# Two mixes in one TensorE call, the decays' products as a call of their own, and new orders on five engines

## The chip, the cores and the metric

The kernel runs on one core of one Trainium2 chip. The metric is device time in microseconds (us): the median of several runs. The profile comes from one more execution. TensorE is PE in the rows (PEld its weight loads), VectorE DVE, ScalarE ACT, GpSimd POOL, SyncE SP.

## The reference

A cross-attention block without softmax on x and a context (8 batches of 256 rows of 512 columns), followed by an RWKV block with a recurrent state of 32 heads of 16:

```python
g_x = conv1x1(g_w, g_b, ctx); theta_x = conv1x1(theta_w, theta_b, x); phi_x = conv1x1(phi_w, phi_b, ctx)
y = (theta_x^T phi_x / N) g_x^T ; x = batchnorm(conv1x1(w_w, w_b, y)) + x
xa = ln(x); sx = shifted(xa) - xa
t = tanh((xa + sx * maa_x) @ maa_w1).reshape(B, L, 5, 32)
mw, mk, mv, mr, mg = t_j @ maa_w2[j]                  # the five "mixes"
xw, xk, xv, xr, xg = xa + sx * (maa_j + m_j)
w = exp(-exp(time_decay + tanh(xw @ decay_w1) @ decay_w2))
r, k, v = xr @ Wr.T, xk @ Wk.T, xv @ Wv.T ; g = silu(xg @ Wg.T)
step: out = r (faaaa * k v^T + s) ; s = k v^T + w * s    # over 256 positions
x = x + groupnorm(out) * g @ Wo.T
xc = ln(x) ; x = x + sigmoid(xr2 @ fWr.T) * (square(relu(xk2 @ fWk.T)) @ fWv.T)
```

All operands are float32, and every weight and activation stays float32 on TensorE.

## The kernel before

Each batch goes through three parts, and the names of the calls say which: a_ (the attention block, the first layer norm, the five mixes and the products with Wk, Wv, Wr, Wg), b_ (the recurrence) and c_ (Wo, the second layer norm and the last three products). The parts are pipelined: in a round of the steady part, TensorE works on a_phi_g to a_x1 of a coming batch, on the mixes and products of batch b1, on the recurrence of b2 and on c_ of b3 and b4. Rounds run for i = 3 to 7; before them stands fill(), behind them drain(). Nothing is scheduled by a planner: each engine has fill, iteration and drain written out by hand as a list of calls, each call waits on semaphores, and an engine runs its list strictly in that order. So a call that waits holds back all that stands behind it on its engine.

The recurrence works inside blocks of 16 positions by doubling (h = 1, 2, 4, 8). Each batch has 17 chunks g of 128 x 512 products: 0 and 1 are the diagonal, 2 is h = 1, 3 and 4 are h = 2, 5 to 8 are h = 4, 9 to 16 are h = 8. VectorE makes the products of chunks 0 to 2 (b_prod), GpSimd those of 3 to 16; three buffers of prod hold them. TensorE sums each by a matmul with ones16 into one of the two halves of CH (b_chunks), VectorE weighs the half with v (b_weigh) and reduces it. Between two values of h, VectorE multiplies RA by the decays (b_update_r) and GpSimd multiplies K (b_update_k). For these, b_wprod makes the products of decays over 2, 4 and 8 positions and over the block (wprod, wblock): four VectorE instructions, called inside b_chunks at g == 1.

A mix is four matmuls with 32 rows of maa_w2 (for mix g of low_w) and 32 rows of tanh values: step m takes row group m for column tiles 0 and 1, and row group (m + 2) % 4 for tiles 2 and 3 (MIX_ROWS), in the order 0, 2, 1, 3. All five mixes go to PSUM tensor PA. VectorE adds maa and multiplies by sx into xmix (a_mix on VectorE, mix_scaled), GpSimd adds xa (a_mix on GpSimd, mix_ready). a_ranks leaves its result in PB, from which ScalarE takes the tanh (tmix_ready). a_decay and a_decay2, the two products of the decays, write PB too.

At the start TensorE runs keep_warm (four matmuls on zeros, inside a_phi_g(0, 0)), the first half of the context's product (a_phi_g), setup (the transposition of the output weights, which needs bn_s from GpSimd and the scaling by VectorE), and the second half. ScalarE's setup scales Wo by a half. In the last batch the calls b_sums, b_reads, c_turn_y, c_wo, c_turn and c_key have a keep_warm ahead of them.

In the rows one float32 matmul is two records (LDWEIGHTS and MATMUL each), so that "x8" is four matmuls.

Of the kernel before, what the change touches and what calls it, by code (L numbers as in the profile page):

```python
# [10 lines left out]
P = 128  # L11
# [10 lines left out]
def build_xattn_rwkv(nc, x_d, ctx_d, shift_d, s0_d, chan_d, bnv_d, theta_b_d, pgb_d, thetaT_d, pgT_d, ww_d,  # L22
                     maa_w1_d, maa_w2_d, dec_w1_d, low_w_d, square_d, ident_d, ones16_d, half_d, out_d):
    B, L, C = x_d.shape
# [6 lines left out]
    DM, DD = 32, 64  # L31
# [16 lines left out]
    with ExitStack() as ctx:  # L48
# [216 lines left out]
        def _(sp):  # L265
# [64 lines left out]
            def fill():  # L330
                keep_x1(0)
                load_ahead_ctx(2)
                load_ahead_ctx(3)
                keep_x1(1)
                load_ahead_x(2)
                load_x(1)
                keep_x1(2)
                load_ahead_x(3)
                keep_x1(3)

            def iteration(i):
# [3 lines left out]
                load_ctx(f1)  # L345
                keep_x1(f2)
                bring_x1(b4)
                load_x(b1)

            def drain():  # L350
                store(4)
# [4 lines left out]
                keep_x1(7)  # L356
# [10 lines left out]
        def _(pe):  # L367
# [114 lines left out]
            def a_mix(a, step):  # L482
                if a is None:
                    return
                if step == 0:
                    pe.wait_ge(tmix_ready, 7 * (a + 1))
                else:
                    pe.wait_ge(mix_scaled, 10 * a + 2 * step)
                for ct in [0, 2, 1, 3]:
                    g, w2, t = MIX_ROWS[step][ct // 2]  # L490
                    rows = slice(DM * g, DM * (g + 1))
                    mm = pe.matmul(PA[:, ct * L:(ct + 1) * L], w2[rows, MIX_COL[step][ct] * P:(MIX_COL[step][ct] + 1) * P],  # L492
                                   t[rows], start=True, stop=True)
                mm.then_inc(mix_mm, 1)

# [14 lines left out]
            def a_decay(a):  # L510
                if a is None:
                    return
                pe.wait_ge(mix_ready, 10 * a + 2)
                for kt in range(CT):
# [220 lines left out]
            def fill():  # L735
                a_phi_g(0, 0)
                setup(0)
# [10 lines left out]
                a_wa(1)  # L748
                a_x1(1)
                a_ranks(0)  # L750
                a_mix(0, 0)
# [3 lines left out]
                a_mix(0, 1)  # L755
                a_decay2(0)
                a_att(2)
# [5 lines left out]
                a_mix(0, 3)  # L763
                a_value(0, 0)
# [5 lines left out]
                a_receptance(0, 1)  # L770
                a_receptance(0, 2)
                a_receptance(0, 3)
                a_theta(2)
                b_chunks(0, 0, 2)
                a_gate(0, 0)
                a_wa(2)
                b_chunks(0, 2, 3)
                a_turn(1)
                a_gate(0, 1)
                a_gate(0, 2)  # L780
                b_chunks(0, 3, 5)
                a_gate(0, 3)
                a_x1(2)
                b_chunks(0, 5, 6)
                a_ranks(1)
                b_chunks(0, 6, 8)
                a_mix(1, 0)
# [1400 lines left out]
```

## Time and profile before

| | us |
|---|---|
| median of 3 runs | 906.08 |
| lowest, highest | 904.01, 906.25 |
| the profiled execution | 905.25 |
| its span, first to last instruction | 903.2 |
| TensorE busy in the span | 861.3 (95%) |
| VectorE busy | 626.5 (69%) |
| ScalarE busy | 352.0 (39%) |
| GpSimd busy | 298.7 (33%) |
| TensorE's mean granted clock | 0.994 of full |

A timeline row reads: start in us, time from start to end, engine, line, operation, output <- inputs, shapes, count of records, and in brackets the idle time before it and who ended it. Matmuls are pipelined, so a group of them ends some 0.16 us after the next can start.

### The profile page before, as it was taken

To read this page: it belongs to the slowest core of one execution; us is meant where nothing else is said; L and a number is where in the kernel's file an instruction comes from. 1 tells how busy PE (TensorE), PEld (TensorE's weight loads), DVE (VectorE), ACT (ScalarE), POOL (GpSimd) and SP (SyncE) were. 2 spreads that over 40 slices of the span, in tenths; PEclk is the share of its full clock that TensorE was granted. 3 is DMA by queue.
4 is the path that set the end of the run, shared out by engine and by line. 5 is a ranking of instruction groups with operands and counts; after the bars stand their busy time and mean duration, and the time that the engine had idled before them with its cause. 6 is when DMAs were issued, how large, how long until landed. Compare 5 with 4: busy or idle time off the path is not lost. (4 is left out here: it accounts for less than half of the span.)

```text
span 903.2 us, 16352 instructions
## 1 busy us (share of the span) xinstructions
PE 861.3 (95%) x6490; PEld 583.7 (65%) x6490; DVE 626.5 (69%) x1110; ACT 352.0 (39%) x715; POOL 298.7 (33%) x281
## 2 busy tenths in 40 slices
PE   6699999899999999999998999999999999999997
PEld 4477568557764776557764686647866577368674
DVE  1465966897589926997379954899369966995341
ACT  1222145633462146433362343621464147236422
POOL 2043632373107520274105720166202831640000
PEclk9999999999999999999999999999999999999999
DMA  9730111000011000300003000020001000010010
GB/s 308 296 94 1 46 56 41 1 1 1 2 42 53 1 3 1 117 1 1 1 1 116 1 2 2 27 91 1 2 1 47 1 2 1 1 48 3 16 56 24
DMA packets 17020, 34.09 MB, mean 38 GB/s; under 512 B 2224, under 2 KB 3888, under 8 KB 16944
## 3 DMA queue, kind: packets, MB, share of 16 engines
q1 hardware_dynamic: 14048, 31.20, 10.1%
q10 hardware_dynamic: 2896, 1.84, 0.7%
q8 instruction: 52, 0.85, 0.4%
q14 instruction: 24, 0.20, 0.1%
HBM read 24.65 MB, written 8.39 MB: 37 GB/s over the span
## 5 line engine op out<-in xcount | busy, mean ns | idle before, releaser
L586 PE MATMUL CH<-prod,ones 128*128 128x512 f32 x272 | 140.2, 610 | 17.6 <-DVE av L1637 7.2
L2030 POOL TENSOR_TENSOR xmix<-xmix,xa 128x512 f32<-128x512 f32 x80 | 94.0, 1196 | 185.0 <-DVE xmix L1545 185.0
L2040 POOL TENSOR_TENSOR prod<-RA,K 128x512 f32<-128x512 f32 x112 | 133.5, 1214 | 51.1 <-DVE RA L1607 31.1
L1545 DVE SCALAR_TENSOR_TENSOR xmix<-PA,chan,sx 128x256 f32<-128x256 f32 x160 | 66.1, 475 | 57.5 <-PE PA L492 57.5
L1219 ACT ACTIVATE st<-av,half 32x512 f32<-32x512 f32 x64 | 74.6, 1166 | 40.0 <-DVE av L1682 38.6
L586 PEld LDWEIGHTS CH<-prod,ones 128*128 128x128 f32 x272 | 46.0, 189 | 59.2 <-issue 33.1
L1637 DVE TENSOR_TENSOR av<-CH,vT 128x512 f32<-128x512 f32 x112 | 76.4, 682 | 7.6 <-PE CH L586 7.0
L1643 DVE TENSOR_REDUCE yred<-av 128x64 f32<-128x512 f32 (+2 forms) x112 | 76.9, 686 | 3.9
L498 PE MATMUL PC<-sqb,sq_fWk 128*128 128x256 f32 x256 | 59.9, 381 | 0.9 <-DVE sqb L1761 0.9
L680 PE MATMUL PC<-sq_Wo,y 128*128 128x512 f32 x128 | 60.3, 601 | 0.3 <-DVE y L1725 0.3
L498 PEld LDWEIGHTS PB<-xmix,sq_Wk 128*128 128x128 f32 x256 | 48.5, 190 | 17.9 <-issue 12.4
L498 PE MATMUL PB<-xmix,sq_Wk 128*128 128x256 f32 x256 | 59.9, 379 | 0.0
L498 PE MATMUL PB<-xmix,sq_Wg 128*128 128x256 f32 x256 | 59.9, 382 | 0.0
L498 PE MATMUL PB<-xmix,sq_Wr 128*128 128x256 f32 x256 | 59.4, 383 | 0.0
L505 PE MATMUL PC<-sq_fWv,kk 128*128 128x512 f32 x128 | 59.0, 597 | 0.0
L498 PE MATMUL PB<-xmix,sq_Wv 128*128 128x256 f32 x256 | 58.9, 383 | 0.0
L505 PE MATMUL PC<-sq_fWr,sxc 128*128 128x512 f32 x128 | 58.2, 594 | 0.0
L498 PEld LDWEIGHTS PC<-sqb,sq_fWk 128*128 128x128 f32 x256 | 48.3, 190 | 14.2 <-issue 7.2
L2052 POOL TENSOR_TENSOR K<-K,W 128x512 f32<-128x512 f32 x8 | 12.0, 1498 | 137.5 <-DVE prod L1575 137.5
L498 PEld LDWEIGHTS PB<-xmix,sq_Wr 128*128 128x128 f32 x256 | 47.8, 190 | 13.0 <-issue 7.3
L498 PEld LDWEIGHTS PB<-xmix,sq_Wg 128*128 128x128 f32 x256 | 47.4, 190 | 11.1 <-issue 5.7
L498 PEld LDWEIGHTS PB<-xmix,sq_Wv 128*128 128x128 f32 x256 | 47.4, 190 | 8.2 <-issue 2.0
(162 smaller groups left out, 1397.0 us busy)
## 6 DMA issues: line engine op xcount, KB each, us to landing
x<-x_rows SPq DMA_DIRECT2D x11, 512.0 KB, 3.9
x<-in_x SPq DMA_DIRECT2D x8, 512.0 KB, 4.0
x_rows<-x SPq DMA_DIRECT2D x8, 512.0 KB, 5.2
out_x<-x SPq DMA_DIRECT2D x8, 512.0 KB, 3.0
ctx_t<-in_ctx SPq DMA_DIRECT2D x5, 512.0 KB, 4.9
y<-in_ctx SPq DMA_DIRECT2D x3, 512.0 KB, 8.2
sq_Wk<-in_square SPq DMA_DIRECT2D x1, 1024.0 KB, 13.3
sq_Wv<-in_square SPq DMA_DIRECT2D x1, 1024.0 KB, 16.7
```

Of the source, the lines that this page charges most:

```text
L498: mm = pe.matmul(out[:, mt * L:(mt + 1) * L], w[:, kt, mt * P:(mt + 1) * P], rhs[:, kt, :], start=(kt == 0), stop=(kt == CT - 1))
L505: mm = pe.matmul(out[:, t * C:(t + 1) * C], lhs[:, kt, t * P:(t + 1) * P], w[:, kt, :], start=(kt == 0), stop=(kt == CT - 1))
L586: pe.matmul(CH[:, (g % 2) * CHUNK:(g % 2 + 1) * CHUNK], ones16[:], prod[:, g % 3, :], start=True, stop=True).then_inc(chunk_mm, 1)
L680: mm = pe.matmul(PC[:, t * C:(t + 1) * C], y[:, t * C + kt * P:t * C + (kt + 1) * P], sq_w["Wo"][:, kt, :], start=(kt == 0), stop=(kt == C ...
L1219: act.activation(st[p, :, :, 32 * q:32 * q + S], src, ACT.Copy, scale=half[p, 0:1]).then_inc(st_ready, 1)
L1545: i = dve.scalar_tensor_tensor(xmix[:, SLOT_OF[name], ct, :], PA[:, ct * L:(ct + 1) * L], vec("maa_" + name, ct), sx[:, ct, :], ALU.add, A ...
L1637: dve.tensor_tensor(by_pair(dst, h), by_pair(src, h), v, ALU.mult).then_inc(av_ready, 1)
L1643: dve.tensor_reduce(yred[:, c * n:(c + 1) * n], by_pair(dst, h), AX.X, ALU.add).then_inc(red_ready, 1)
L2030: pool.tensor_tensor(m, m, xa[:, ct:ct + 2, 1:L + 1], ALU.add).then_inc(mix_ready, 1)
L2040: pool.tensor_tensor(by_pair(prod[:, g % 3, :], h), r, k, ALU.mult).then_inc(prod_pool, 1)
L2052: pool.tensor_tensor(ke, ke, wfactor(h, 1), ALU.mult).then_inc(K_up, 1)
```

## The change

1. a_first_mixes replaces TensorE's a_mix(., 0) and a_mix(., 1): mix w goes to PA as before, mix k to PB, and the eight matmuls are issued so that four follow each other on four different row groups. VectorE's a_mix takes step k from PB.
2. a_decay, which writes PB, waits in addition until VectorE has read both mixes (mix_scaled).
3. b_wprod is a call of its own in VectorE's list, in a round ahead of b_prod(b2, 0), and no longer inside b_chunks.
4. The lists of all five engines have another order in many places: among them TensorE's setup(0) ahead of a_phi_g(0, 0), a_ranks ahead of chunk 0, ScalarE's a_xa(0) ahead of a_att(1), VectorE's c_shift behind chunk 13, GpSimd's mix sums, and SyncE's context loads behind those of x.

```diff
@@ tensor @@
             def a_mix(a, step):
                 if a is None:
                     return
-                if step == 0:
-                    pe.wait_ge(tmix_ready, 7 * (a + 1))
-                else:
-                    pe.wait_ge(mix_scaled, 10 * a + 2 * step)
+                pe.wait_ge(mix_scaled, 10 * a + (2 if step == 2 else 2 * step))
                 for ct in [0, 2, 1, 3]:
-                    g, w2, t = MIX_ROWS[step][ct // 2]
-                    rows = slice(DM * g, DM * (g + 1))
-                    mm = pe.matmul(PA[:, ct * L:(ct + 1) * L], w2[rows, MIX_COL[step][ct] * P:(MIX_COL[step][ct] + 1) * P],
-                                   t[rows], start=True, stop=True)
+                    mm = mix_columns(PA, step, ct)
                 mm.then_inc(mix_mm, 1)
+
+            def mix_columns(out, step, ct):
+                g, w2, t = MIX_ROWS[step][ct // 2]
+                rows = slice(DM * g, DM * (g + 1))
+                return pe.matmul(out[:, ct * L:(ct + 1) * L], w2[rows, MIX_COL[step][ct] * P:(MIX_COL[step][ct] + 1) * P],
+                                 t[rows], start=True, stop=True)
+
+            def a_first_mixes(a):
+                if a is None:
+                    return
+                pe.wait_ge(tmix_ready, 7 * (a + 1))
+                for lo in range(2):
+                    for out, step in [(PA, 0), (PB, 1)]:
+                        for ct in [lo, lo + 2]:
+                            mm = mix_columns(out, step, ct)
+                        if lo:
+                            mm.then_inc(mix_mm, 1)
...
                 pe.wait_ge(mix_ready, 10 * a + 2)
+                pe.wait_ge(mix_scaled, 10 * a + 4)
...
             def fill():
+                setup(0)
                 a_phi_g(0, 0)
-                setup(0)
                 a_phi_g(0, 1)
...
+                a_ranks(0)
                 a_x1(1)
-                a_ranks(0)
-                a_mix(0, 0)
+                a_first_mixes(0)
@@ scalar @@
                 setup(0)
+                a_xa(0)
                 a_att(1)
                 a_theta(1)
-                a_xa(0)
@@ vector @@
+                src = PB if name == "k" else PA
                 for ct in range(CT):
-                    i = dve.scalar_tensor_tensor(xmix[:, SLOT_OF[name], ct, :], PA[:, ct * L:(ct + 1) * L],
+                    i = dve.scalar_tensor_tensor(xmix[:, SLOT_OF[name], ct, :], src[:, ct * L:(ct + 1) * L],
...
                 for g in range(lo, hi):
-                    if g == 1:
-                        b_wprod(u)
```

The orders that matter most, as the programs have them. First TensorE's beginning, up to the first attention product, before and then changed (keep_warm writes CH, setup turns tmix into PB, a_phi_g writes PA from ctx_t):

```order
1 L371 MATMUL CH<-dec 128x256 x4
2 L394 MATMUL PA<-pgT,ctx_t 128x256 x4
3 L732 MATMUL PB<-ident,tmix 128x128 x2
4 L394 MATMUL PA<-pgT,ctx_t 128x256 x4
5 L405 MATMUL PA<-zbuf 128x128 x4
```

```order
1 L744 MATMUL PB<-ident,tmix 128x128 x2
2 L371 MATMUL CH<-dec 128x256 x4
3 L394 MATMUL PA<-pgT,ctx_t 128x256 x8
4 L405 MATMUL PA<-zbuf 128x128 x4
```

The transposition came between the halves of the context's product and is now ahead of all.

TensorE in the first third of a round, from the turn of y (c_turn_y), before and then changed (CH<-prod is a chunk, PB<-zbuf a_ranks, PC<-sq_Wo c_wo, PB<-xmix,dec_w a_decay, PB<-dec a_decay2):

```order
277 L652 MATMUL PC<-ident,y 128x128 x4
278 L586 MATMUL CH<-prod,ones 128x512
279 L652 MATMUL PC<-ident,y 128x128 x4
280 L586 MATMUL CH<-prod,ones 128x512 x2
281 L473 MATMUL PB<-zbuf,maa_w 128x256 x4
282 L477 MATMUL PB<-zbuf,maa_w 32x128 x8
283 L586 MATMUL CH<-prod,ones 128x512
284 L680 MATMUL PC<-sq_Wo,y 128x512 x2
285 L492 MATMUL PA<-tmix,maa_w 128x256 x4
286 L680 MATMUL PC<-sq_Wo,y 128x512 x2
287 L586 MATMUL CH<-prod,ones 128x512 x2
288 L680 MATMUL PC<-sq_Wo,y 128x512 x2
```

```order
268 L664 MATMUL PC<-ident,y 128x128 x4
269 L473 MATMUL PB<-zbuf,maa_w 128x256 x4
270 L477 MATMUL PB<-zbuf,maa_w 32x128 x8
271 L598 MATMUL CH<-prod,ones 128x512 x2
272 L664 MATMUL PC<-ident,y 128x128 x4
273 L493 MATMUL PA<-tmix,maa_w 128x256 x2
274 L493 MATMUL PB<-tmix,maa_w 128x256 x2
275 L493 MATMUL PA<-tmix,maa_w 128x256 x2
276 L493 MATMUL PB<-tmix,maa_w 128x256 x2
277 L598 MATMUL CH<-prod,ones 128x512 x2
278 L692 MATMUL PC<-sq_Wo,y 128x512 x4
279 L598 MATMUL CH<-prod,ones 128x512 x2
```

The ranks are ahead of all chunks instead of behind the third, and the double mix stands before chunk 2; mix w alone stood between two parts of c_wo. In both lists a_decay comes next but is followed before by mix k (row 291) and c_wo, now by c_wo and a_decay2.

VectorE at the start of a round's recurrence, before and then changed (gate is a_gate, prod<-RA,chan,K products 0 and 1, xc and x c_out, yint<-CH the weighing of chunks 0 and 1, wprod and wblock b_wprod, RA<-RA,W b_update_r):

```order
388 L1556 SCALAR_TENSOR_TENSOR gate<-gate,PB 128x512 x2
389 L1569 SCALAR_TENSOR_TENSOR prod<-RA,chan,K 128x256 x4
390 L1780 SCALAR_TENSOR_TENSOR xc<-xc,PC 128x512
391 L1782 SCALAR_TENSOR_TENSOR x<-xc,x 128x512
392 L1575 TENSOR_TENSOR prod<-RA,K 128x512
393 L1623 TENSOR_TENSOR yint<-CH,vT 128x512
394 L1592 TENSOR_TENSOR wprod<-W 128x512
395 L1592 TENSOR_TENSOR wprod<-wprod 128x256
396 L1592 TENSOR_TENSOR wprod<-wprod 128x128
397 L1590 TENSOR_TENSOR wblock<-wprod 128x4x16
398 L1607 TENSOR_TENSOR RA<-RA,W 128x512
399 L1623 TENSOR_TENSOR yint<-CH,vT 128x512
```

```order
392 L1565 SCALAR_TENSOR_TENSOR gate<-gate,PB 128x512 x2
393 L1603 TENSOR_TENSOR wprod<-W 128x512
394 L1603 TENSOR_TENSOR wprod<-wprod 128x256
395 L1603 TENSOR_TENSOR wprod<-wprod 128x128
396 L1601 TENSOR_TENSOR wblock<-wprod 128x4x16
397 L1578 SCALAR_TENSOR_TENSOR prod<-RA,chan,K 128x256 x4
398 L1789 SCALAR_TENSOR_TENSOR xc<-xc,PC 128x512
399 L1791 SCALAR_TENSOR_TENSOR x<-xc,x 128x512
400 L1734 TENSOR_TENSOR y<-y,gate 128x512
401 L1584 TENSOR_TENSOR prod<-RA,K 128x512
402 L1634 TENSOR_TENSOR yint<-CH,vT 128x512
403 L1618 TENSOR_TENSOR RA<-RA,W 128x512
```

The four instructions on the decays moved from behind product 2 to ahead of product 0, and the first c_gate (y<-y,gate) ahead of product 2.

## Rows read from the trace of the kernel before

**Rows 1.** Windows: length, each engine's busy time (instructions), granted clock, DMA share, GB/s.

```profile
479.98:585.25 105.27, 102.98 (x797) 69.77 (x796) 77.72 (x138) 43.38 (x90) 36.67 (x35) 1.00 0.08 26
...
41.92:49.83 7.91, 7.91 (x24) 5.75 (x25) 1.66 (x4) 0.00 (x0) 2.31 (x2) 0.58 0.00 0
```

**Rows 2.** Groups by line, TensorE: busy us, mean ns, idle before and releasers.

```profile
L586 PE MATMUL CH<-prod,ones 128*128 128x512 f32 x272 | 140.2, 610 | 17.6 <-DVE av L1637 7.2 <-POOL prod L2040 6.6 <-DVE prod L1569 2.7
```

**Rows 3.** Timeline of TensorE in a round: chunk 3, mix w, c_wo, chunk 6.

```profile
484.93 1.12 PE L586 MATMUL CH<-prod,ones 128*128 128x512 f32 x2 [0.75 <-POOL prod L2040]
...
487.70 1.13 PE L492 MATMUL PA<-tmix,maa_w 32*128 32x256 f32 x8
488.76 1.98 PE L680 MATMUL PC<-sq_Wo,y 128*128 128x512 f32 x4
...
495.51 1.10 PE L586 MATMUL CH<-prod,ones 128*128 128x512 f32 x2 [1.33 <-DVE av L1637]
```

**Rows 4.** Timeline of TensorE, the first 15 us.

```profile
1.24 3.41 PE L371 MATMUL CH<-dec 128*128 128x256 f32 x8 [1.24 <-DVE dec L1821]
6.03 1.97 PE L394 MATMUL PA<-pgT,ctx_t 128*128 128x256 f32 x8 [1.38 <-DMA pgT<-in_pgT]
11.35 0.66 PE L732 MATMUL PB<-ident,tmix 128*128 128x128 f32 x2 [3.36 <-DVE bn_tmp L1792]
11.81 3.17 PE L394 MATMUL PA<-pgT,ctx_t 128*128 128x256 f32 x8
```

**Rows 5.** Timeline of ScalarE in the fill, 30 to 35 us.

```profile
30.06 1.91 ACT L1282 ACTIVATE sq_Wo<-sq_Wo 128x2048 f32<-128x2048 f32 x1 [10.16 <-DMA sq_Wo<-in_square]
...
32.70 1.93 ACT L1067 ACTIVATE xa<-PA,chan 128x256 f32<-128x256 f32 x4
```

**Rows 6.** Timeline of TensorE in the fill, 32 to 50 us.

```profile
32.19 0.70 PE L431 MATMUL PC<-wwT,sxc 128*128 128x256 f32 x2 [1.50 <-ACT sxc L1054]
...
36.48 1.99 PE L473 MATMUL PB<-zbuf,maa_w 128*128 128x256 f32 x8 [1.04 <-DVE zbuf L1526]
...
41.92 2.08 PE L492 MATMUL PA<-tmix,maa_w 32*128 32x256 f32 x8 [2.44 <-ACT tmix_g L1079]
43.92 5.97 PE L394 MATMUL PC<-pgT,y 128*128 128x256 f32 x16
```

**Rows 7.** Timeline of VectorE in a round, to the first c_gate, and c_shift.

```profile
475.39 1.67 DVE L1569 SCALAR_TENSOR_TENSOR prod<-RA,chan,K 128x256 f32<-128x256 f32 x4
477.59 0.69 DVE L1780 SCALAR_TENSOR_TENSOR xc<-xc,PC 128x512 f32<-128x512 f32 x1 [0.53 <-PE PC L505]
...
478.92 0.69 DVE L1575 TENSOR_TENSOR prod<-RA,K 128x512 f32<-128x512 f32 x1
...
480.12 1.70 DVE L1592 TENSOR_TENSOR wprod<-W 128x512 f32<-128x512 f32 x1
...
482.78 0.68 DVE L1607 TENSOR_TENSOR RA<-RA,W 128x512 f32<-128x512 f32 x1
...
483.99 1.43 DVE L1725 TENSOR_TENSOR y<-y,gate 128x512 f32<-128x512 f32 x1
...
510.93 1.50 DVE L1757 TENSOR_TENSOR sxc<-xc 128x1024 f32<-128x1024 f32 x1
512.47 2.36 DVE L1761 SCALAR_TENSOR_TENSOR sqb<-sxc,chan,xc 128x256 f32<-128x256 f32 x4
```

**Rows 8.** Timeline of GpSimd in a round: K's update, products 3 and 4, mix sum.

```profile
479.77 1.50 POOL L2052 TENSOR_TENSOR K<-K,W 128x512 f32<-128x512 f32 x1 [18.26 <-DVE prod L1575]
483.60 2.95 POOL L2040 TENSOR_TENSOR prod<-RA,K 128x512 f32<-128x512 f32 x2 [2.33 <-DVE RA L1607]
...
492.49 2.31 POOL L2030 TENSOR_TENSOR xmix<-xmix,xa 128x512 f32<-128x512 f32 x2 [1.41 <-DVE xmix L1545]
```

**Rows 9.** Timeline of TensorE at the last batch's chunks 3 and 5.

```profile
776.60 1.13 PE L586 MATMUL CH<-prod,ones 128*128 128x512 f32 x2 [0.39 <-POOL prod L2040]
...
781.47 1.12 PE L586 MATMUL CH<-prod,ones 128*128 128x512 f32 x2 [1.17 <-POOL prod L2040]
```

## What is predicted, and from what

> **What bounds the kernel now.** I read the windows first. A steady round of the pipeline lasts 105.27 us and TensorE is busy for 102.98 of it at the full clock, VectorE for 77.72 [rows 1]. So TensorE is the bound, and a round can only gain by less work on it or by its waits. The groups by line say where it waits: 17.6 us before the chunk matmuls, for VectorE's reading of the chunks, GpSimd's products and VectorE's [rows 2]. In a round two places make up nearly all of the 2.3 us that are left: 0.75 us before chunk 3, for GpSimd's product, and 1.33 us before chunk 6, for VectorE [rows 3]. The rest is the two ends. At the start TensorE waits until 11.35 us for the scaled output weights [rows 4], then from one engine's latency to the next up to 41.92 us, and after a wait of 2.44 us its clock falls to 1.2 GHz: of 41.92 to 49.83 us the mean granted clock is 0.58 [rows 1, 6].
>
> **The mixes.** One call of four 32-row matmuls (eight records) occupies TensorE from 487.70 to 488.76 us, 1.06 us [rows 3]; its two row groups run side by side, the other two lie idle. The new call puts the first two mixes, eight matmuls, on four groups. Low end: nothing saved, if only two groups run at a time, since no row of before shows four at this width. High end: 1.06 us, if the pair lasts as long as one call. I take 1.06, the row nearest to it: the call is made of the same stream, with groups that share nothing. No reason makes the pair longer than two calls, so there is no loss. Eight batches: -8.5 us.
>
> The Trainium skill (TensorE: Matmul & The Clock Gate, Part 3) gives 3.07 times, not 4, for four row groups at K=32 and 512 columns; by that figure the pair would last a tenth of a microsecond longer, an estimate of +0.5 us in all. No trace here shows it.
>
> **The start.** The transposition of the output weights now stands ahead of the four warming matmuls (3.41 us) and of both halves of the first context product. These used to fill the wait that ends at 11.35 us; now they follow it. Most of the warming runs at 1.2 GHz (0.43 us a record, as before), so it takes 3.0 us; the product's two halves then take 3.5 us at full clock instead of 3.17 for the second alone [rows 4]. TensorE is 3.4 us late at 15 us. It is given back: batch 1's chain had waits of 1.50 us (ScalarE scaled Wo until 31.97) and 1.04 us, ScalarE now puts xa(0) ahead of att(1), and the second a_x1 moves into the wait for the tanh [rows 5, 6]. Walked through, xa(0) starts at 32.4 us instead of 32.70, a_ranks(0) at 36.3 instead of 36.48, a_x1(1) runs from 39.1 to 40.9, and the mixes start at 41.7: -0.2 us. And TensorE then waits 0.8 us there instead of 2.44, so I take the clock to stay at 2.4 GHz: the mix costs 1.06 us instead of 2.00, and the context product 3.5 instead of 5.91: -3.4 us. Bounds of that: 0, if the clock falls all the same, and -3.4.
>
> **The middle.** I walk a round in the new order with the old durations, in us from the first c_turn_y (477.38 before). VectorE: products of the decays 2.66 (480.12 to 482.78), first products 1.6, c_out 1.33 (two rows of 0.69, start to start with what follows), c_gate 1.4 [rows 7]; product 2 is there at 5.6. GpSimd updates K until 7.3, and TensorE can take its first product 1.33 us after it started [rows 3, 8]: chunk 3 at 8.7. TensorE, with the ranks ahead of chunk 0 and the double mix behind, is there at 7.7: a wait of 0.9. Before the double mix it waits 0.3 for ScalarE's tanh. Next, a_decay has a new wait, since mix k lies in PB, which it overwrites: VectorE has read it at 15.2. But GpSimd, behind product 5, ends the sum of mix w (2.3 us) [rows 8] only at 15.9, and TensorE stands there at 14.9: 1.1. Behind this wait are queued c_wo, a_decay2 and chunk 6. Then 0.35 before chunk 12, and 1.0 before c_key, because c_shift (3.83 us) [rows 7] now comes after chunk 13 instead of chunk 10. That is 3.7 us of lost slots, 2.9 as the trace counts idle time, against 2.3: +0.6 a round, and four rounds make +2.4. The old waits go; the ones named are late next. The first round (b2 = 1) has no c_out to hide behind: its 2.7 us before chunk 0 [rows 2] becomes some 1.8, a new 1.2 appears in a_gate for mix g, and the others are as above: +1.3.
>
> **The drain.** With batch 6, VectorE goes through its 17 chunks without a pause, so TensorE's shorter mix is waited away again before b_turn_k: +1.1. For batch 7 the decays' products leave the chain, and 0.39 and 1.17 us before its chunks [rows 9] shrink: -1.2, with -1.6 and 0 as bounds. The last chain from the sums to the output has the same pieces, with two c_key ahead of the turn of K in place of behind: 0, within 1 us, covered by c_receptance. SyncE's moved loads (contexts behind x, keep_x1(7) earlier) are wanted tens of microseconds later: 0.
>
> **Sum.** -8.5 - 3.4 - 0.2 + 1.3 + 2.4 + 1.1 - 1.2 = -8.5 us. The profiled execution is 905.25 us, so 896.7; the median of the three runs, 906.08, is 0.8 higher, so I say 897.0.
>
> **Rivals.**
> A. Four groups don't overlap, the pair costs 2.1 us. For it: no row shows four. Against: two do so at no cost. 897.0 + 8.5 = 905.5, no change.
> B. The start isn't given back. If the tanh arrives 3.4 us late and the clock falls again, 897.0 + 3.4 + 3.4 = 903.8. For it: the walk hangs on ScalarE's order, where att(1) now stands behind xa(0). Against: 2.5 us of waits that only reappear if all of them are chained.
> C. Slower: the decays' products stand in front of the first chunk product. It decides as soon as TensorE arrives at chunk 0 before VectorE does; my walk leaves 1.7 us (product 0 ready at 1.55, TensorE at 3.3). If VectorE's gate comes later by more than that, each round pays up to 2.66 us [rows 7], five rounds 13.3: 910. Against: VectorE idles 0.53 us there now [rows 7], and ranks (2.7 us) cover the rest.
> D. Better: the waits that I found are hidden and the longer start of batch 1 gains as well. My walk of the fill gave another 2.5 us which I left out; with half of the waits gone, 889.
> That the table moves nothing is excluded by the order of instructions.
>
> **Numbers.** Forecast 897.0, 0.62; A 0.10; B 0.10; C 0.08; D 0.10. Range 889.5 to 904.5: it takes in B, half of D and the bounds of the unknown costs (0 to -3.4 for the clock, +-1 us a round for four walked rounds). A change of 0.3% (2.7 us) is about what a measurement of this kernel can tell from none. Faster than 903.4: forecast, D and a part of B, 0.77; within 0.3%: A and the rest of B, 0.14; slower: C and a tail, 0.09.
>
> **What would show it.** In PE's timeline the sixteen records of the double mix last 1.06 us (A: 2.1). The granted clock of 40 to 50 us is 1.0, and the mixes begin at 41.7 (B). Chunk 0 follows the ranks with no wait on VectorE's products (C). In a round the waits are before the double mix, chunk 3 (GpSimd), a_decay (GpSimd's xmix) and c_key (VectorE's sqb); a round lasts 104.8 us. I am wrong if a round is over 105.3 us, or if the clock still falls at 41.7 us.

## The result, and the profile after

| | before | after |
|---|---|---|
| median | 906.16 us (904.01 to 906.7, 4 runs) | 880.88 us (880.46 to 881.46, 4 runs) |
| ratio | | 0.9726, 95% interval 0.9709 to 0.9743 |
| the profiled execution | 905.25 us | 881.46 us |
| TensorE busy | 861.3 us | 846.3 us |
| VectorE, GpSimd busy | 626.5, 298.7 us | 613.3, 290.9 us |

The change gains 25 us. The forecast was 9 (897.0, range 889.5 to 904.5), so the direction held and the size did not. Among all the runs of this document two single executions, 2242 us in longer_products and 4955 us in scale_later, took several times as long as the others of their kernel, for a reason that no run shows; they move the two medians by some 0.2 us and leave scale_later without a trace to read. The stages below run from one first record of b_reads to the next in TensorE's timeline, the last one to the last matmul; the forecast column puts my terms where they belong.

| stage | before | after | change | forecast |
|---|---|---|---|---|
| fill | 152.6 | 147.6 | -5.0 | -0.2 - 3.4 - 2 x 1.06 = -5.7 |
| round i = 3 | 93.6 | 92.2 | -1.4 | +1.3 - 1.06 = +0.2 |
| round i = 4 | 106.8 | 102.5 | -4.4 | -0.5 |
| rounds 5 to 7, each | 105.27 | 102.45 | -2.8 | +0.6 - 1.06 = -0.5 |
| drain | 229.9 | 225.3 | -4.6 | +1.1 - 1.2 - 1.06 = -1.2 |

Between the two traces 23.8 us are gained where my terms make 8.5; the four rounds 4 to 7 hold 11 of the 15 us between them, the drain 3.4. (Round 4 before has one more wait, 1.34 us in b_sums, that the other rounds lack.) A round of after, as [rows 1] (length, TensorE busy, its weight loads, VectorE, ScalarE, GpSimd, clock, DMA share, GB/s):

```profile
463.80:566.24 102.44, 101.41 (x797) 69.30 (x796) 75.85 (x138) 43.68 (x89) 35.69 (x34) 1.00 0.08 27
```

Busy time fell by 1.57 us and idle time from 2.3 to 1.03. The group that had 17.6 us of waits in [rows 2]:

```profile
L598 PE MATMUL CH<-prod,ones 128*128 128x512 f32 x272 | 135.2, 602 | 1.7 <-DVE av L1648 1.4 <-POOL prod L2053 0.3
```

TensorE's timeline where [rows 3] stood:

```profile
469.57 0.48 PE L493 MATMUL PA<-tmix,maa_w 32*128 32x256 f32 x2
469.59 0.48 PE L493 MATMUL PB<-tmix,maa_w 32*128 32x256 f32 x2
...
470.33 0.38 PE L493 MATMUL PA<-tmix,maa_w 32*128 32x256 f32 x2
470.34 0.38 PE L493 MATMUL PB<-tmix,maa_w 32*128 32x256 f32 x2
470.65 1.98 PE L598 MATMUL CH<-prod,ones 128*128 128x512 f32 x4
472.47 3.60 PE L692 MATMUL PC<-sq_Wo,y 128*128 128x512 f32 x8
475.90 1.88 PE L598 MATMUL CH<-prod,ones 128*128 128x512 f32 x4
478.71 1.09 PE L528 MATMUL PB<-xmix,dec_w 128*64 128x128 f32 x16 [0.93 <-POOL xmix L2043]
```

The sixteen records of the pair start four at a time, 0.02 us apart, and the next call starts 1.08 us after them: one call's time for two. Chunks 2 and 3 (470.65) and 4 and 5 (475.90) follow with no wait. The only wait above 0.1 us in a steady round is the 0.93 before a_decay.

VectorE and GpSimd, as [rows 7] and [rows 8]:

```profile
461.80 0.69 DVE L1603 TENSOR_TENSOR wprod<-W 128x512 f32<-128x512 f32 x1
...
466.36 0.69 DVE L1734 TENSOR_TENSOR y<-y,gate 128x512 f32<-128x512 f32 x1
466.96 0.69 DVE L1584 TENSOR_TENSOR prod<-RA,K 128x512 f32<-128x512 f32 x1
...
468.83 1.04 DVE L1618 TENSOR_TENSOR RA<-RA,W 128x512 f32<-128x512 f32 x1
...
474.49 0.68 DVE L1618 TENSOR_TENSOR RA<-RA,wprod 128x512 f32<-128x512 f32 x1
...
487.22 0.53 DVE L1755 TENSOR_SCALAR sqb<-x,mv,rstd 128x512 f32<-128x512 f32 x1
...
492.95 1.00 DVE L1755 TENSOR_SCALAR sqb<-x,mv,rstd 128x512 f32<-128x512 f32 x1
...
499.14 1.21 DVE L1766 TENSOR_TENSOR sxc<-xc 128x1024 f32<-128x1024 f32 x1
500.39 1.67 DVE L1770 SCALAR_TENSOR_TENSOR sqb<-sxc,chan,xc 128x256 f32<-128x256 f32 x4
```

```profile
467.81 1.50 POOL L2065 TENSOR_TENSOR K<-K,W 128x512 f32<-128x512 f32 x1 [20.22 <-DVE prod L1584]
470.00 2.49 POOL L2053 TENSOR_TENSOR prod<-RA,K 128x512 f32<-128x512 f32 x2 [0.68 <-DVE RA L1618]
472.72 1.29 POOL L2065 TENSOR_TENSOR K<-K,wprod 128x512 f32<-128x512 f32 x1 [0.23 <-POOL prod L2053]
...
491.31 5.70 POOL L2053 TENSOR_TENSOR prod<-RA,K 128x512 f32<-128x512 f32 x5
```

This is where the forecast and the trace part. wprod<-W lasts 0.69 us; in [rows 7] it lasted 1.70. The first y<-y,gate lasts 0.69; there it lasted 1.43. In both traces every VectorE instruction that lasts over 0.15 us more than the shortest of its kind has a GpSimd instruction beside it, and the long tensor_tensor of 512 columns end some 0.55 us after it. wprod<-W of before starts at 480.12, 0.35 us into K<-K,W, which ends at 481.27; it ends at 481.82. RA<-RA,W here starts at 468.83 beside K<-K,W, which ends at 469.31, and ends at 469.87. So I read the long ones not as slow but as standing still until GpSimd is nearly done, and then taking their 0.69 us. Those with both inputs in SBUF do this. av<-CH,vT (one input in PSUM) does not, with a mean of 681 ns over 112 in after, and yred<-av (one input) neither, with 686. But one input is no safe sign: the TENSOR_SCALAR sqb<-x,mv,rstd, with x alone as a full input, lasts 0.53 us with GpSimd idle (487.22) and 1.00 beside GpSimd's products (492.95). The Trainium skill (SBUF — State Buffer, Who interferes with whom) says of two inputs just that: a VectorE instruction with two SBUF inputs contends with a GpSimd instruction that reads SBUF, and who starts first has the shared ports to its end. The traces agree, in both directions: GpSimd's products 3 and 4 take 2.49 us here and 2.95 in [rows 8], where y<-y,gate of [rows 7] ran in between.

The start, as [rows 4] and [rows 6], and ScalarE, as [rows 5]:

```profile
11.55 0.66 PE L744 MATMUL PB<-ident,tmix 128*128 128x128 f32 x2 [11.55 <-DVE bn_tmp L1801]
12.01 3.62 PE L371 MATMUL CH<-dec 128*128 128x256 f32 x8
15.42 4.41 PE L394 MATMUL PA<-pgT,ctx_t 128*128 128x256 f32 x16
21.14 1.16 PE L405 MATMUL PA<-zbuf 128*128 128x128 f32 x8 [1.32 <-DVE zbuf L1475]
...
37.74 1.99 PE L473 MATMUL PB<-zbuf,maa_w 128*128 128x256 f32 x8 [0.94 <-DVE zbuf L1534]
...
43.18 0.48 PE L493 MATMUL PA<-tmix,maa_w 32*128 32x256 f32 x2 [0.54 <-ACT tmix_g L1087]
...
44.26 3.72 PE L394 MATMUL PC<-pgT,y 128*128 128x256 f32 x16
```

```profile
30.30 1.91 ACT L1290 ACTIVATE sq_Wo<-sq_Wo 128x2048 f32<-128x2048 f32 x1 [5.56 <-DMA sq_Wo<-in_square]
...
33.96 1.92 ACT L1075 ACTIVATE xa<-PA,chan 128x256 f32<-128x256 f32 x4
```

TensorE comes 4.8 us late to the first attention product (16.30 before), the mixes 1.3 us late, and the context product behind them runs at full clock (3.72 us instead of 5.97). ScalarE's xa(0) is as late as the mixes (33.96 against 32.70).

The last batch's chunks 3 and 5, as [rows 9]; both waits are gone:

```profile
755.53 1.02 PE L598 MATMUL CH<-prod,ones 128*128 128x512 f32 x2
...
762.39 1.02 PE L598 MATMUL CH<-prod,ones 128*128 128x512 f32 x2
```

### The profile page after: what moved, and what is told of

Its sections match the earlier page's. It is cut to its first block, busy times and chain, and to the rows that moved or that the text cites. A ratio compares the mean times of both kernels' runs of the same rounds, so it can differ in the third digit from the quotient of the medians.

```text
span 879.4 us, 16360 instructions
## 1 busy us (share of the span) xinstructions
PE 846.3 (96%) x6490; PEld 578.6 (66%) x6490; DVE 613.3 (70%) x1110; ACT 354.1 (40%) x715; POOL 290.9 (33%) x281
## 4 chain that ended last, share of the span: by engine, by line
PE 84%; DVE 6%; issue 3%; ACT 3%; POOL 1%; DMA 1%; ACTq 0%; DVEq 0%; POOLq 0%
PE PB L509 24%; PE PC L516 13%; PE CH L598 9%; PE PC L509 6%; PE PC L692 4%; PE PA L493 4%; PE CH L657 3%; PE CH L634 3%; PE PB L371 2%; PE PA L394 2%; PE PB L473 2%; PE CH L452 2%; DVE xmix L1554 1%; PE PC L394 1%; PE PC L664 1%
## 5 line engine op out<-in xcount | busy, mean ns | idle before, releaser
L2043 POOL TENSOR_TENSOR xmix<-xmix,xa 128x512 f32<-128x512 f32 x80 | 96.7, 1230 | 170.1 <-DVE xmix L1554 170.1
L2053 POOL TENSOR_TENSOR prod<-RA,K 128x512 f32<-128x512 f32 x112 | 127.0, 1152 | 40.5 <-DVE RA L1618 32.4
L598 PE MATMUL CH<-prod,ones 128*128 128x512 f32 x272 | 135.2, 602 | 1.7 <-DVE av L1648 1.4
L1554 DVE SCALAR_TENSOR_TENSOR xmix<-PA,chan,sx 128x256 f32<-128x256 f32 x128 | 52.9, 475 | 35.3 <-PE PA L493 33.0
L598 PEld LDWEIGHTS CH<-prod,ones 128*128 128x128 f32 x272 | 47.9, 189 | 43.6 <-issue 31.3
L509 PEld LDWEIGHTS PB<-xmix,sq_Wk 128*128 128x128 f32 x256 | 48.1, 190 | 17.6 <-issue 12.5
```

The lines of the kernel that those rows point to most:

```text
L509: mm = pe.matmul(out[:, mt * L:(mt + 1) * L], w[:, kt, mt * P:(mt + 1) * P], rhs[:, kt, :], start=(kt == 0), stop=(kt == CT - 1))
L598: pe.matmul(CH[:, (g % 2) * CHUNK:(g % 2 + 1) * CHUNK], ones16[:], prod[:, g % 3, :], start=True, stop=True).then_inc(chunk_mm, 1)
L1554: i = dve.scalar_tensor_tensor(xmix[:, SLOT_OF[name], ct, :], src[:, ct * L:(ct + 1) * L], vec("maa_" + name, ct), sx[:, ct, :], ALU.add, ...
L2043: pool.tensor_tensor(m, m, xa[:, ct:ct + 2, 1:L + 1], ALU.add).then_inc(mix_ready, 1)
L2053: pool.tensor_tensor(by_pair(prod[:, g % 3, :], h), r, k, ALU.mult).then_inc(prod_pool, 1)
```

## The experiments

| kernel | median us | a round (i = 6), us |
|---|---|---|
| before (beside them) | 905.1 to 905.7 | 105.27 |
| after | 880.9 | 102.45 |
| mix_one_by_one | 881.0 | 102.46 |
| mix_apart | 884.6 | 102.69 |
| wprod_inside | 888.9 | 103.64 |
| orders_only | 892.9 | 103.64 |
| before_wprod | 902.6 | 104.65 |
| before_mix | 949.6 | 111.82 |
| before_small_K, after_small_K | 887.8, 874.0 | 103.04, 101.63 |
| longer_products | 889.2 | 104.05 |
| gate_back | 880.7 | 102.56 |
| decay_later, decay_later_x2 | 882.2, 882.0 | 102.83, 102.66 |
| mix_apart_decay_later | 886.1 | 102.96 |
| setup_between | 881.2 | 102.46 |
| scale_later, scale_later_v, mix_w_shared | 879.8, 881.9, 882.2 | -, 103.23, 103.06 |

### What the double mix is worth

In the order of issue of mix_one_by_one all of mix w stands ahead of all of mix k:

```diff
-                for lo in range(2):
-                    for out, step in [(PA, 0), (PB, 1)]:
-                        for ct in [lo, lo + 2]:
+                for out, step in [(PA, 0), (PB, 1)]:
+                    for ct in [0, 2, 1, 3]:
```

> The changed kernel with the two first mixes still in one call, but issued one mix after the other, so that two row groups run side by side and not four. If the pair on four groups is worth one call (1.06 us) and TensorE is the bound everywhere, the sixteen records last 2.1 us instead of 1.08 and the kernel takes 880.9 + 8 x 1.06 = 889.4 us. If waits of the new order take up the longer call (the 0.93 us before a_decay in five rounds), it is only some 885.

880.99 us: neither. TensorE's timeline:

```profile
468.36 0.48 PE L493 MATMUL PA<-tmix,maa_w 32*128 32x256 f32 x2
468.39 0.48 PE L493 MATMUL PB<-tmix,maa_w 32*128 32x256 f32 x2
...
469.45 1.13 PE L596 MATMUL CH<-prod,ones 128*128 128x512 f32 x2
```

In the records mix k's first matmuls start 0.03 us after mix w's first, though four matmuls of mix w were issued ahead of them, and the pair takes 1.09 us. The four row groups run together without the interleaved order; here it was enough that the two calls follow each other and share neither rows nor output. So this kernel did not take the overlap away, and mix_apart does it with work in between:

```diff
-                a_first_mixes(b1)
-                b_chunks(b2, 2, 4)
+                a_first_mix(b1, 0)
+                b_chunks(b2, 2, 3)
+                a_first_mix(b1, 1)
+                b_chunks(b2, 3, 4)
```

> The changed kernel with mix k issued behind the next piece of work (chunk 2, in the fill and the drain what follows there) instead of together with mix w, so that the two calls can't overlap: 8 x 1.06 us more work for TensorE. If every microsecond of TensorE's work counts, 880.9 + 8.5 = 889.4 us. My theory: in five rounds TensorE waits 0.93 us before a_decay for GpSimd's sum of mix w, whose moment does not depend on it, and the longer mix fills that wait: 5 x 0.13 + 3 x 1.06 = +3.8, 884.7 us.

884.59 us, as the theory said. TensorE's busy time in a round is 102.59 us instead of 101.41, and the wait before a_decay is gone from rounds 4 to 7:

```profile
472.15 1.13 PE L493 MATMUL PA<-tmix,maa_w 32*128 32x256 f32 x8
473.21 1.13 PE L595 MATMUL CH<-prod,ones 128*128 128x512 f32 x2
474.27 1.13 PE L493 MATMUL PB<-tmix,maa_w 32*128 32x256 f32 x8
...
481.54 1.09 PE L525 MATMUL PB<-xmix,dec_w 128*64 128x128 f32 x16
```

The pair saves 1.06 us of work eight times, but in the rounds TensorE then waits 0.93 us longer for GpSimd: of 8.5 us 3.7 reach the end. By stages of the two traces the fill has 2.2 us of it (149.8 against 147.6), rounds 4 to 7 have 0.24 each and the drain, though a pair stands there too, 0.2 (225.5 against 225.3).

before_mix gives the kernel before the double mix and a_decay's second wait, and no new order:

> The kernel before with only the double mix (and a_decay's wait for the reading of mix k), all orders as they were. TensorE has 8 x 1.06 = 8.5 us less work: 897.7 us if nothing else changes. But VectorE reads mix k only behind chunk 6, which TensorE issues right ahead of a_decay; a_decay then waits for VectorE from 496.5 to some 499.5 us of the old trace, 2.9 us in each of five rounds: theory 906.2 - 8.5 + 5 x 2.9 = 912 us. If the wait is hidden, 898.

949.6 us, 44 slower. The wait is where it was expected, and longer than the 2.9 us that I had given it:

```profile
527.03 1.98 PE L528 MATMUL PB<-xmix,dec_w 128*64 128x128 f32 x16 [5.00 <-DVE xmix L1554]
```

TensorE waits 5.00 us until VectorE, behind the weighing up to chunk 6, has read mix k, and a_decay runs at half clock after that (1.98 us instead of 1.09). The eight such waits come to 35.4 us, where I had expected five of 2.9, and the granted clock is 0.5 for 55.5 us of the span behind the start, against 11.6 in before. Alone the edit is a large loss; in the changed kernel, where VectorE reads mix k behind chunk 3, it is a gain.

### The products of the decays, and the orders

wprod_inside puts the four instructions back into b_chunks at g == 1:

```diff
                 for g in range(lo, hi):
+                    if g == 1:
+                        b_wprod(u)
...
-                b_wprod(b2)
                 b_prod(b2, 0)
```

> The changed kernel with the four products of the decays back inside b_chunks at g == 1, beside GpSimd's update of K. Theory (a VectorE instruction with both inputs in SBUF and GpSimd's instruction exclude each other): the first of the four takes 1.7 us again instead of 0.69, VectorE comes to product 5's RA and to mix w about 2.5 us later, TensorE's idle time in a round rises from 0.93 to 2.3 us or more, and the kernel takes 880.9 + 5 x 1.4 = 888 us. Rival (the new orders alone took the waits away, the place of the four does nothing): the first of them lasts 0.69 us and the kernel takes 881 +-1 us.

888.9 us: the size is right, the mechanism half. wprod<-W takes 0.68 us here, since it comes as K<-K,W is ending (574.09 and 574.20 us). But the four now stand between product 2 and RA, so product 3 comes 1.3 us later, and RA of h = 2 meets the second update of K:

```profile
577.87 1.13 PE L598 MATMUL CH<-prod,ones 128*128 128x512 f32 x2 [0.84 <-POOL prod L2051]
```

```profile
579.82 1.78 DVE L1618 TENSOR_TENSOR RA<-RA,wprod 128x512 f32<-128x512 f32 x1
```

A round is 1.2 us longer than in after, and the drain 3.3 us (228.6 against 225.3).

before_wprod moves them ahead of product 0 in the kernel before:

> The kernel before with only the four products of the decays moved ahead of product 0 on VectorE. Theory of the exclusion: the first of them takes 0.69 us instead of 1.70; product 2 comes some 0.9 us later and TensorE may wait up to 0.7 us for it, but the 0.75 us before chunk 3 and most of the 1.33 us before chunk 6 go: a round 1.0 to 1.5 us shorter, 906.2 - 5 x 1.2 = 900 us. Rival (my rival C: they stand in front of the first chunk and TensorE waits for it): a round up to 2.7 us longer, 906 to 919 us. Rival (the place does nothing alone): 906.

902.6 us (ratio 0.9975, 0.9964 to 0.9987), less than forecast. wprod<-W takes 0.69 us, but in the old order VectorE comes late to c_out (0.36 us before the second c_turn_y) and to the weighing of chunk 0 (0.44 us before chunk 2), RA<-RA,W stands beside K<-K,W instead (1.70 us), and the first round waits 4.37 us before chunk 0 instead of 2.73: my rival C, in the round with no c_out.

orders_only undoes both named parts (mix_apart and wprod_inside together; mix k still goes to PB):

> The changed kernel with both named parts undone: mix w and mix k apart, and the products of the decays inside b_chunks. What is left of the gain belongs to the orders. If the parts add up: 880.9 + 3.7 (mixes apart) + 8.0 (decays inside) = 892.6 us, 12.7 under the kernel before. If the longer mix fills waits that the decays' place makes, less: 889 to 892. If the orders are worth nothing alone: 905.

892.89 us. The parts add up: the orders are worth 12.2 us, the place of the decays' products 8.3 (892.9 to 884.6) or 8.0 (888.9 to 880.9), the double mix 3.7 or 4.0. By stages the orders give 2.8 us in the fill, 0.3 in round 3, 3.2 in round 4, 1.6 in each later round and 1.3 in the drain. So over 20 of 24 us come from the orders and the decays' place; all but the fill's 2.8, which I had put at 3.6, lie in the rounds and the drain, which I had walked through and priced at a net loss of 3.6 us. Which of the many moved calls carry the orders' share was not taken apart.

### What made my walk wrong

before_small_K and after_small_K cut GpSimd's updates of K to one pair of columns:

```diff
-                pool.tensor_tensor(ke, ke, wfactor(h, 1), ALU.mult).then_inc(K_up, 1)
+                pool.tensor_tensor(ke[:, 0:1], ke[:, 0:1], wfactor(h, 1)[:, 0:1], ALU.mult).then_inc(K_up, 1)
```

> The kernel before with GpSimd's updates of K cut to the first pair of columns (its outputs are not the reference's for that reason; the instruction and its signals stay). VectorE's first product of the decays waits for nothing that GpSimd does at that place. Theory of the exclusion: with GpSimd's 1.50 us gone from beside it, wprod<-W falls from 1.70 to 0.69 us, and RA<-RA,wprod (h = 2) from 1.77 to 0.69; y<-y,gate stays at 1.43 (it is beside product 3); a round is over 1 us shorter. Rival (the instruction costs 1.70 us by its own shape): both durations stay.

887.8 us. The row of before that [rows 7] doesn't reach, and then VectorE's rows in the round of before_small_K:

```profile
487.02 1.77 DVE L1607 TENSOR_TENSOR RA<-RA,wprod 128x512 f32<-128x512 f32 x1
```

```profile
469.89 0.68 DVE L1592 TENSOR_TENSOR wprod<-W 128x512 f32<-128x512 f32 x1
...
472.73 1.43 DVE L1725 TENSOR_TENSOR y<-y,gate 128x512 f32<-128x512 f32 x1
...
475.77 0.68 DVE L1607 TENSOR_TENSOR RA<-RA,wprod 128x512 f32<-128x512 f32 x1
```

An edit on GpSimd takes 1.02 and 1.09 us off two VectorE instructions that wait for none of these updates, and leaves the third, beside product 3, at 1.43. That shows that the extra time is GpSimd's doing.

> The changed kernel with GpSimd's updates of K cut to the first pair of columns, as in before_small_K (outputs not the reference's for that reason). There the cut was worth 17.4 us. Theory: the changed kernel has already moved most of VectorE's work away from these updates, so the cut is worth only the wait before a_decay and little else: 881 - 5 = 876 us. Rival (the cut is worth its own GpSimd time wherever it stands): 864 us.

873.98 us: 6.9 off, against 17.4 (one run each). What GpSimd's updates cost the end was 17 us before and is 7 after. Since the smaller update also makes products come earlier, neither is the exclusion alone.

longer_products puts my mistake back as work: two reductions on VectorE, as long as what I had counted too much.

```diff
+                    if h == 1:
+                        for lo, hi in [(0, 64), (64, 96)]:
+                            dve.tensor_reduce(spare[:, lo:hi], W[:, 0:16 * (hi - lo)].rearrange("p (n s) -> p n s", s=16), AX.X, ALU.add)
```

> The changed kernel with two extra reductions on VectorE (1024 and 512 columns into a spare tile) ahead of the products of the decays. They add some 1.75 us, the difference between what my walk of a round took (2.66 for the products, 1.43 for the first c_gate) and what these instructions last in the changed kernel. Theory (the wrong durations made the forecast waits): product 2 comes at 5.6 us after the first c_turn_y as in the walk, TensorE waits some 0.9 us for chunk 3 and 1 us or more before a_decay, a round lasts 104.0 to 104.8 us and the kernel 881 + 5 x 1.9 = 890 us or more. Rival (VectorE has slack there, the forecast failed elsewhere): a round stays within 0.5 us of 102.45, under 884 us.

889.2 us. The trace is that of the same kernel run once more (888.5 us):

> The kernel longer_products once more, for its profile. Theory: product 2 is made 5.6 us after the first c_turn_y, TensorE waits 0.9 us before chunk 3 for GpSimd's product and 1 us or more before a_decay, a round is 103.9 to 104.8 us long. Rival: the time lies elsewhere (VectorE's chunks late throughout the round, waits of 0.2 us before many chunks).

```profile
472.06 0.69 DVE L1585 TENSOR_TENSOR prod<-RA,K 128x512 f32<-128x512 f32 x1
...
473.27 1.70 DVE L1622 TENSOR_TENSOR RA<-RA,W 128x512 f32<-128x512 f32 x1
```

```profile
476.42 1.12 PE L599 MATMUL CH<-prod,ones 128*128 128x512 f32 x2 [1.25 <-POOL prod L2057]
...
483.71 1.09 PE L529 MATMUL PB<-xmix,dec_w 128*64 128x128 f32 x16 [1.01 <-POOL xmix L2047]
```

c_turn_y is at 467.19, so product 2 is there at 5.56 us (walk: 5.6), chunk 3 waits 1.25 us (0.9) and a_decay 1.01 (1.1); the round is 104.05 us (104.8). These two waits appear as soon as the assumed time is real: the steps up to them were sound, and their durations were not. The waits before the double mix, chunk 12 and c_key do not appear here either.

gate_back moves one instruction back, the first c_gate behind chunks 0 and 1:

> The changed kernel with one VectorE call back where it was: the first c_gate behind chunks 0 and 1 instead of ahead of them. Theory of the exclusion: y<-y,gate then meets GpSimd's product 3 and takes about 1.4 us instead of 0.69, GpSimd's product 4 waits for it in turn, RA for product 5 comes 0.8 us later and with it GpSimd's sum of mix w, so that the wait before a_decay grows from 0.93 to some 1.7 us: five rounds, +4 us, 885 us. Rival (an instruction moved costs its 0.69 us wherever it stands, and VectorE has slack): 881 +-0.5 us.

```profile
469.20 1.43 DVE L1734 TENSOR_TENSOR y<-y,gate 128x512 f32<-128x512 f32 x1
```

```profile
478.00 1.09 PE L528 MATMUL PB<-xmix,dec_w 128*64 128x128 f32 x16 [1.03 <-POOL xmix L2043]
```

880.74 us: the rival's. The exclusion comes as expected (GpSimd's products 3 and 4 take 2.95 us again instead of 2.49), and costs 0.1 us a round: product 2 came 0.6 us earlier in exchange, and the wait before a_decay grew by 0.1. How long a collision lasts does not say what it costs.

### The one wait left, and the start

decay_later puts c_wo(b3, 1, 0) ahead of a_decay, chunk 6 ahead of a_decay2 and c_gate ahead of mix k; decay_later_x2 also moves c_x2 behind chunk 4; mix_apart_decay_later joins the first with mix_apart.

> The changed kernel with c_wo(b3, 1, 0) ahead of a_decay and chunk 6 ahead of a_decay2 on TensorE, and VectorE's second c_gate ahead of mix k: a_decay comes 1.8 us later, when GpSimd's sum of mix w is there. Theory: the wait of 0.93 us goes in five rounds and nothing takes its place: 880.9 - 4.6 = 876.3 us. Rival: c_gate, now behind GpSimd's products, makes c_wo wait (y is ready 0.2 us before TensorE wants it), or a_decay2's tanh comes late: 880 to 883 us.

> Both edits. If the double mix is worth 1.06 us a batch wherever TensorE has no wait behind it, this kernel is 8.5 us slower than the one with a_decay later alone: 884.8 us, and so as fast as the one with the mixes apart and the wait. If it comes out at 876 to 880, the mixes are hidden by something else.

> decay_later with VectorE's first c_x2 behind the weighing of chunk 4 instead of ahead of it. In decay_later TensorE waited 0.26 us for y and 0.81 us before chunk 6 for VectorE. Theory: chunk 4 is weighed 1.5 us earlier, the 0.81 us go, 0.26 stays: 882.2 - 5 x 0.8 = 878.2 us. Rival: the sum of mix k comes too late because GpSimd's c_rstd stands ahead of it, and TensorE waits before a_key: no gain, 882.

882.2, 886.1 and 882.0 us: no gain. In decay_later two waits take the place of one:

```profile
478.97 1.98 PE L692 MATMUL PC<-sq_Wo,y 128*128 128x512 f32 x4 [0.26 <-DVE y L1734]
480.88 1.09 PE L528 MATMUL PB<-xmix,dec_w 128*64 128x128 f32 x16
482.79 1.10 PE L598 MATMUL CH<-prod,ones 128*128 128x512 f32 x2 [0.81 <-DVE av L1648]
```

In decay_later_x2 the idle time is down to 0.66 us a round (after: 1.03), but the busy time is 102.0 instead of 101.4. A group beside a narrow call occupies TensorE longer (in before, a chunk of two records takes 0.86 us between full-width matmuls, 0.96 behind a narrow call, 1.03 ahead of a_decay and 1.06 between two narrow calls). So part of what an order costs stands in the busy time, and idle time alone does not rank orders that differ by tenths. With a_decay later the double mix is worth 3.8 us (886.1 to 882.2), not 8.5: the new waits give its work back as the old one did. mix_w_shared, built on scale_later (below), gives half of mix w's sum to VectorE:

> scale_later with the second half of the sum of mix w on VectorE instead of GpSimd. VectorE has to wait for GpSimd's update of K right behind it anyway. Theory: the sum is complete 1.2 us earlier, the wait before a_decay falls from 0.93 to some 0.4 us, now for VectorE's reading of mix k, and five rounds give 2.5 us: 877.3 us. Rival: the addition itself meets GpSimd's product and delays RA for product 5, the wait stays: 880 us.

882.2 us: the wait falls to 0.62 us, now for VectorE's reading of mix k, and the round is 0.6 us longer than in after all the same; why was not looked into further.

setup_between puts setup(0) back between the halves of the context product; scale_later also moves ScalarE's scaling of Wo behind a_decay2(0); scale_later_v is scale_later with another order around a_decay in the rounds.

> The changed kernel with the transposition of the output weights back between the halves of the first context product. TensorE starts at 1.2 us and reaches the first attention product at 16.3 instead of 21.1 us. Theory: ScalarE's scaling of Wo, which ends at some 32.2 us whatever TensorE does, then holds xa(0), so the mixes start near 42.0 instead of 43.2 us: -1.2 us if the clock holds, 879.7 us. Rival: TensorE, 3.6 us ahead, waits over 2 us for the tanh, its clock falls to 1.2 GHz as in the kernel before, and 3.4 us are lost: 883 us.

881.2 us. TensorE starts at 1.25 us, the mixes start 0.2 us earlier (43.01) and the kernel gains nothing. Both reasons show in the trace: Wo's scaling ends at 32.2 and TensorE waits for ScalarE, and after that wait the granted clock is 0.5 for 3.4 us, under the ranks (1.99 us in after):

```profile
34.29 0.70 PE L431 MATMUL PC<-wwT,sxc 128*128 128x256 f32 x2 [2.33 <-ACT sxc L1062]
35.93 3.62 PE L473 MATMUL PB<-zbuf,maa_w 128*128 128x256 f32 x8 [0.94 <-DVE zbuf L1534]
```

> setup_between with ScalarE's scaling of Wo, which waits for a DMA until some 30 us, behind a_decay2(0) instead of ahead of xa(0). Theory (that wait holds the chain of batch 0, which is why an earlier TensorE gained nothing): xa(0) follows its turn at some 29 us, the mixes start near 38.5 us instead of 43, 4 us gained if the clock holds: 877 us. Rival: the chain is then held by a weight that lands late, and TensorE waits before the keys or the values instead: 881.

> scale_later, and in the rounds both parts of c_wo(b3, 1) ahead of chunk 6 with a_decay between them, VectorE's c_gate ahead of mix k and its c_x2 behind chunk 4. Theory: of the 0.93 us before a_decay 0.3 is left and the wait of 0.2 before a_decay2 goes too, but each new neighbour of a narrow call costs 0.1: 0.2 us a round less than scale_later, 1 us in all: 876 us. Rival: nothing gained or up to 1 us lost, as in decay_later_x2.

879.8 and 881.9 us. In the trace of scale_later_v the mixes start at 36.96 us instead of 43.18, and then TensorE waits for the context of batch 2:

```profile
41.07 1.22 PE L394 MATMUL PC<-pgT,y 128*128 128x256 f32 x2 [2.96 <-DMA y<-in_ctx]
```

The start is bound by ScalarE's chain and behind it by the contexts as they land: of 6.2 us gained at the mixes 1.6 are left at the end of the fill (145.9 against 147.6), and the rounds, with their other order, are 0.8 us longer each. scale_later (ratio to before 0.9714, 0.9695 to 0.9733) has the lowest time of the kernels that do the whole work, but 0.1% under after is less than these runs can tell apart. I found no version that surely beats the changed kernel.

## Why the prediction was wrong, point by point

- **The mixes, -8.5.** The duration was right: 1.08 us for the pair on four groups, as one call. As a term of the sum it was right only in the fill. In the rounds and the drain the work was saved and mostly waited for: mix_apart shows 3.7 us at the end. The estimate from the Trainium skill (TensorE: Matmul & The Clock Gate, Part 3), a tenth of a microsecond more for the pair, did not show: 1.08 against 1.06 us. (Eight times a tenth would be 0.8 us, not the 0.5 given with it; nothing rests on either.)
- **The start, -0.2 and -3.4.** The clock held, as forecast. TensorE was 4.8 us late, not 3.4: half clock lasted until 17.0 us, into the context product, which I had taken at full clock throughout. Of that 1.3 us were left at the mixes. The sum is -5.0 instead of -5.7 with two mixes: the term was mis-sized by 0.7.
- **The middle, +2.4. This is the step that failed.** The forecast named five waits in a round. Those before the double mix (0.1 came, 0.3 named), chunk 3, chunk 12 and c_key did not come; the one before a_decay did (0.93 us, 1.1 named). What was wrong is the durations that the walk carried from [rows 7] to new places. The walk took 2.66 us for the decays' products and 1.4 for c_gate; at their new places they take 1.65 and 0.60, start to start. Product 2 was there at 3.85 us instead of 5.6, and GpSimd's products came earlier with it. longer_products, with this time put back, has two of the waits (chunk 3 and a_decay) and the forecast round within 0.8 us. c_shift is a second case of the same mistake: the walk took 3.83 us, from rows with GpSimd's products beside them, and behind chunk 13, with GpSimd idle, it takes 2.84 (499.14 to 501.98 us), in after and in longer_products_look; no run puts this time back, so that it made the wait of 1.0 us before c_key is my reading. With 2.9 us of idle time corrected to 1.03 some 0.5 us a round are left, in the busy time: chunks and c_wo occupy 0.7 us less in a round, other groups a little more. I put that down to fewer neighbours of narrow calls; no run isolates it.
- **The first round, +1.3.** It was -0.3 without the mix. The 2.73 us before chunk 0 are gone; in their place TensorE waits 2.03 us before a_ranks, for VectorE's gate, and the ranks then cover the decays' products. In the trace of after the granted clock is 0.5 from 163.8 to 167.2 us behind that wait.
- **The drain, +1.1 and -1.2.** Batch 7's two waits of [rows 9] went as forecast. That the shorter mix is waited away again, the +1.1, is borne out by mix_apart, whose drain is only 0.2 us longer. What was too small is the -1.2: putting the decays' products back (wprod_inside) makes the drain 3.3 us longer, and the orders alone had made it 1.3 shorter (orders_only, 228.6 against 229.9). In all -4.6 against -1.2; TensorE's idle time in the drain is 3.2 us instead of 5.9.
- **The rivals.** A: excluded by the records. B: of its 3.4 us 1.5 came (the mixes at 43.18 against 41.7), and no fall of the clock. C: not in after, where the ranks stand ahead of chunk 0 in every round; it is what before_wprod shows in its first round. D was right in its first half, the waits hidden, and too small: I gave it 0.10 and 889, and took "half of the waits gone" as its end. Its second half, a start that gains another 2.5 us, did not come.
- **The sum and the range.** 896.7 and 0.8 make 897.5, not 897.0; the 0.5 us change nothing. The range allowed +-1 us a round for a walk that took its durations from rows in which GpSimd stood beside VectorE. An error of that kind repeats in every round and in the drain with one sign; the range treated it as a small one.

## What to carry to other kernels

Before a walk takes a duration from a row, look at what the other engine did in that moment: the time of a VectorE instruction beside a GpSimd instruction can be mostly wait, and moved to a quiet place it can take half (0.69 us instead of 1.43 or 1.70 here). Price a saving on the bound engine twice, once as work and once as the moment at which the next input is there; here 8.5 us of saved work were worth 3.7. An overlap that needs a new wait is only as good as the order around it: before_mix lost 44 us with it.

## What the runs showed of the hardware beyond that

- VectorE and GpSimd hold each other up instruction by instruction. A VectorE tensor_tensor of 512 columns with both inputs in SBUF goes from 0.69 us to up to 1.78 and then ends some 0.55 us after GpSimd's; sqb<-x,mv,rstd, with one full input, goes from 0.53 to 1.00 (after). The other way, the K<-K,wprod that takes 1.29 us in a round of after takes 1.78 in longer_products_look.
- In the records TensorE starts matmuls of a later call ahead of earlier ones of the call in front if they use other row groups (mix_one_by_one: 0.03 us after the first).
- TensorE's clock: waits of 2.33 (setup_between), 2.44 (before) and 2.96 us (scale_later_v) stand in front of stretches at 1.2 GHz of 3.4 to 6.8 us. The same wait of 2.03 us before a_ranks stands in the traces of after and of 13 other kernels; in four of the 14 (after, decay_later, decay_later_x2, orders_only) such a stretch begins within 0.6 us of the wait's end, in the others not. The 2.73 us before chunk 0 in before have none behind them, and 1.66 us in before_wprod (from 331.95 us) have one, from 334.76. So the length of the wait alone did not decide it. At the start of before the clock is full from 4.2 us (2.9 us after the first matmul) and half again from 11.0 to 14.4, behind the wait of 3.36 us; in after it is half until 17.0 us, 5.5 us after the first matmul.
